# Narrow attentions: exponents from scores with keys on partitions in place of transposed probabilities

## The reference, cut to what matters

```
s = q k^T * scale + mask        # 256 x keys; keys = 768 in L0 (context and x), 512 in L2 and L3
p = exp(s - rowmax(s)) / rowsum
a = p v                         # 256 x 16
x = x + (a Wo + bias)           # in L2 times tanh(gate)
```

## Time and profile before

| | us |
|---|---|
| median of 3 runs | 1140.93 |
| lowest, highest | 1139.70, 1142.56 |
| profiled execution, span | 1145.1 |
| TensorE busy | 956.2 (84%) |
| TensorE weight loads busy | 806.1 (70%) |
| VectorE busy | 823.1 (72%) |
| ScalarE busy | 606.0 (53%) |
| GpSimd busy | 331.5 (29%) |

### The profile page before, as it was taken

How to read it: one execution, slowest core, us unless ns; L and a number is a source line. 1 busy time by engine, 2 the same in 40 slices (tenths; PEclk the granted TensorE clock), 3 DMA queues, 4 the chain that set the end, 5 groups by cost and what they waited for, 6 DMA issues and landing times. The chain is left out here.

```text
span 1145.1 us, 17853 instructions
## 1 busy us (share of the span) xinstructions
PE 956.2 (84%) x6548; PEld 806.1 (70%) x6548; DVE 823.1 (72%) x1627; ACT 606.0 (53%) x1371; POOL 331.5 (29%) x324
## 2 busy tenths in 40 slices
PE   4788886569999999975999999998586798478958
PEld 3666665557888888963898899887475466465647
DVE  3377757976787887776678878777674587747865
ACT  2488873034555555642455556554424587257842
POOL 4245541441112222004102222200005355525520
PEclk8889998878999999997999999999798699789989
DMA  5985106140001110003101111000304920195120
GB/s 176 234 143 61 16 1 253 46 153 1 21 18 38 38 38 1 1 1 117 38 1 37 38 37 38 1 1 1 116 1 111 177 43 1 51 187 73 21 79 19
DMA packets 38242, 69.49 MB, mean 61 GB/s; under 512 B 7462, under 2 KB 23336, under 8 KB 35596
## 3 DMA queue, kind: packets, MB, share of 16 engines
q1 hardware_dynamic: 38156, 68.35, 24.6%
HBM read 57.31 MB, written 11.02 MB: 60 GB/s over the span
## 5 line engine op out<-in xcount | busy, mean ns | idle before, releaser
L1189 ACT CAST L1a_probsT_hi<-L1a_bank 128x512 fp32r<-128x512 f32 x128 | 68.8, 589 | 92.6 <-PE L1a_bank L1085 92.6
L1043 POOL TENSOR_SCALAR L1a_wo_hi<-L1a_stage 128x512 fp32r<-128x512 f32 x16 | 11.3, 707 | 347.8 <-PE L1a_sums L84 336.8
L1279 DVE TENSOR_REDUCE L1a_top<-L1a_scores 128x2 f32<-128x1024 f32 x64 | 78.2, 1222 | 35.2 <-PE L1a_scores L84 35.2
L1215 ACT ACTIVATE L1a_probs<-L1a_scores,L1a_neg_max 128x512 f32<-128x512 f32 x128 | 86.8, 684 | 30.3 <-DVE L1a_bias_shifted L1283 24.7
L82 PE MATMUL L1a_bank<-L1a_probsT_hi,L1a_v_hi 128*128 128x256 f32 x256 | 72.5, 283 | 11.7 <-DVE L1a_probsT_lo L1238 11.0
L1238 DVE TENSOR_TENSOR L1a_probsT_lo<-L1a_bank,L1a_probsT_hi 128x512 fp32r<-128x512 f32 x128 | 81.9, 681 | 0.1
L1191 ACT ACTIVATE L1a_attended_hi<-L1a_bank,L1a_cols 128x256 fp32r<-128x256 f32 x64 | 30.3, 474 | 91.5 <-PE L1a_bank L84 91.5
L82 PE MATMUL L1a_bank<-L1a_w_hi,ctxT_hi 128*128 128x256 f32 x256 | 75.7, 296 | 0.0
L83 PE MATMUL L1a_bank<-L1a_w_lo,ctxT_hi 128*128 128x256 f32 x256 | 73.1, 286 | 0.0
L84 PE MATMUL L1a_bank<-L1a_w_hi,ctxT_lo 128*128 128x256 f32 x256 | 73.0, 285 | 0.0
L400 POOL TENSOR_SCALAR L0a_probs<-L0a_probs,L0a_inverse 128x768 f32<-128x768 f32 x64 | 57.2, 906 | 53.2 <-DVE L0a_inverse L651 53.2
(11 more groups left out here) (407 smaller groups left out, 3157.9 us busy)
## 6 DMA issues: line engine op xcount, KB each, us to landing
L1a_stage<-in_L_w SPq DMA_DIRECT2D x14, 1024.0 KB, 4.8
L0m_fold_wq<-in_L_wq SPq DMA_DIRECT2D x2, 2048.0 KB, 20.4
L0a_k_stack<-L0a_k_dram SPq DMA_DIRECT2D x12, 192.0 KB
L0a_w_qkv<-L0a_k_dram SPq DMA_DIRECT2D x12, 192.0 KB
L0a_probs<-in_L_wo SPq DMA_DIRECT2D x1, 2048.0 KB, 10.0
L0a_probsT<-in_L_wo SPq DMA_DIRECT2D x1, 2048.0 KB, 11.2
L0m_stage<-in_L_wm SPq DMA_DIRECT2D x4, 512.0 KB, 6.0
L0m_fold_bias_k<-in_L_bias_k SPq DMA_DIRECT2D x2, 1024.0 KB, 16.0
```

Of the source, the lines that this page charges most:

```text
L1189: nc.scalar.copy(out, source).then_inc(ring.hi_done, 1)
L1215: nc.scalar.activation(probs[:, g % 2, qt, :], scores[:, qt, :], ACT.Exp, bias=neg_max[:, g % 2, qt:qt + 1], accum_out=row_sum[:, g % 2, q ...
L1279: link(nc.vector.tensor_reduce(top[:, :], scores[:, :, :], AX.X, ALU.max))
```

## The change

The 32 heads are handled as 16 *pairs* (`NP`), two of them a unit. For each pair TensorE makes the scores twice. *Row scores* (`row_scores`) have queries on partitions as before, but contract 64 rows for each head of the pair, into two banks of a pair; VectorE takes the maxima of both heads in one instruction and nothing else uses them. *Exponents* (`exponents`) have keys on partitions: k_stack is the stationary operand, q_stack (256 queries) the moving one. The two rows 64a+33 and 64a+34 of q_stack hold the negated maxima's high and low part, against ones in k_stack, so the maximum is subtracted within the matmul, and the mask row comes the same way. ScalarE takes the exponential of 1024 elements at once, straight into `probsT`, as `product_v` reads it. The unused columns of `v` hold ones, so the product has the row sums in its row 16; after it come a copy (`take_sums`), a shuffle and a reciprocal (`invert_sums`), a product on GpSimd, and the high and low parts.

The maxima of a unit are split in high and low part, transposed (`turn_maxima`), copied, and brought into q_stack by four DMAs of two partitions. Row scores run four pairs ahead (`LEAD`). All four octets have k and q stacks of their own, and GpSimd clears each half separately; in L0a the fourth k stack still lies over w_qkv. `probsT` for two of four pairs lies over kT. PSUM: two banks for v jobs, maxima, V products and outputs (`late`), and three pairs of banks shared in turn by row scores and exponents. Two of the v jobs stay ahead, the others go between the first row scores; output blocks 0 and 1 go into the loop (`OUT_STEP`). The wide weights for the bias values are loaded in three pieces instead of two.

```diff
-        score_slots, probs_slots, small_slots = (4, 8, 8) if nk == S else (2, 6, 8)
-        probs = ph.sb("probs", [P, probs_slots, nk])
+        kept = 3 if cfg["bias_values"] else 4
+        stacks = [place(f"k_stack{o}", [P, 4, nk], F32R) for o in range(kept)]
+        if kept < OCTETS:
+            stacks.append(place("k_stack3", [P, 4, nk], F32R, at=at_w))
+        q_stack, _ = place("q_stack", [P, OCTETS, 4, Q], F32R)
+        banks = ph.psum(2)
+        pairs_banks = [ph.ctx.enter_context(nc.psum_tensor(f"{name}_pair{i}", [P, 2, 512], F32)) for i in range(3)]
+        ring = ph.ring([*banks, pairs_banks[2][:, 0, :], pairs_banks[2][:, 1, :]])
+        late = Ring(banks, ph.sem, "late")
...
+        STEPS = range(-LEAD, NP + 1)
+        def rows_of(s):
+            return [(s + LEAD, qt, c) for qt in range(2) for c in range(MC)] if s + LEAD < NP else []
+        def exps_of(s):
+            return [(s, h) for h in range(HALVES)] if 0 <= s < NP else []
+        def turned(s):
+            m = s + LEAD
+            return m // 2 - 1 if m % 2 == 0 and 2 <= m <= NP else None
+        def summed_up(s):
+            return s // 2 - 1 if s % 2 == 0 and s >= 2 else None
...
             for o in range(OCTETS):
...
                 sp.wait_ge(written[o], 64 if o else 80)
-                sp.wait_ge(cleared[r], 3)
-                if o >= 2:
-                    sp.wait_ge(scores_full, 16 * (o - 1))
+                sp.wait_ge(cleared[o], 6)
...
+            for u in range(UNITS):
+                late.wait_evacuated(sp, late_job["N", u])
+                for i in range(4):
+                    tt, a = divmod(i, 2)
+                    o, t = divmod(2 * u + tt, 4)
+                    row = 64 * a + 33
+                    sp.dma_start(raw(q_stack[row:row + 2, o, t, :]), maximaT[2 * i:2 * i + 2, u % 2, :]).then_inc(maxima_loaded[u % 2], 16)
...
+            def clear(o):
+                if o == 3 and kept < OCTETS:
+                    pool.wait_ge(late.full, late_job[v_jobs[-1]] + 1)
                 for a in range(2):
+                    half = np.s_[64 * a + 32:64 * a + 64]
+                    settled(nc.gpsimd.memset(raw(q_stack[half, o, :, :]), 0.0), cleared[o], 3 * a + 1)
+                    settled(nc.gpsimd.memset(raw(k_stack[o][half, :, :]), 1.0), cleared[o], 3 * a + 2)
+                    settled(nc.gpsimd.memset(raw(q_stack[64 * a + 32:64 * a + 33, o, :, :]), 1.0), cleared[o], 3 * a + 3)
+            clear(0)
+            settled(nc.gpsimd.memset(v[:, :, :], 1.0), values_set, 1)
+            settled(nc.gpsimd.memset(maxima[:, :, :, :], 0.0), maxima_clear, 1)
+            if cfg["bias_values"]:
+                pool.wait_ge(late.full, late_job["bias_values"] + 1)
+            for o in range(1, OCTETS):
+                clear(o)
+            for u in range(UNITS):
+                pool.wait_ge(inverted, 2 * u + 2)
...
+                nc.gpsimd.tensor_tensor(scaled[:, u % 2, :], summed[:, u % 2, :], inverse[:, u % 2, :],
+                                        ALU.mult).then_inc(scaled_ready, 1)
...
+            def row_scores(item):
...
+                wait_pair_free(pe, item)
+                for a in range(2):
+                    last = nc.tensor.matmul(pair_bank(item)[:, a, 0:CW], q_stack[64 * a:64 * a + 64, o, t, qt * P:(qt + 1) * P],
+                                            k_stack[o][64 * a:64 * a + 64, t, c * CW:(c + 1) * CW], start=True, stop=True)
+                last.then_inc(rows_full, 1)
+            def exponents(item):
...
+                if h == 0 and p % 2 == 0:
+                    pe.wait_ge(maxima_loaded[u % 2], 64 * (u // 2 + 1))
+                wait_pair_free(pe, item)
+                for kk in range(2):
+                    at = (2 * h + kk) * P
+                    for a in range(2):
+                        last = nc.tensor.matmul(pair_bank(item)[:, a, kk * Q:(kk + 1) * Q], k_stack[o][64 * a:64 * a + 64, t, at:at + P],
+                                                q_stack[64 * a:64 * a + 64, o, t, :], start=True, stop=True)
+                last.then_inc(exps_full, 1)
...
+            for s in STEPS:
+                for k in range(max(len(rows_of(s)), len(exps_of(s)), 1)):
+                    for item in rows_of(s)[k:k + 1]:
+                        row_scores(item)
+                    for item in exps_of(s)[k:k + 1]:
+                        exponents(item)
+                    if k == 0:
+                        for item in values_of(s):
+                            values(item)
+                        if turned(s) is not None:
+                            turn_maxima(turned(s))
+                        if summed_up(s) is not None:
+                            product_v(summed_up(s))
+                if s in (OUT_STEP, OUT_STEP + 1):
+                    output(s - OUT_STEP)
...
+                        nc.scalar.activation(probsT[p % 4][:, :, h * 512:(h + 1) * 512], pair_bank((p, h))[:, :, :],
+                                             ACT.Exp).then_inc(pair_freed((p, h)), 1)
...
+                nc.vector.tensor_reduce(parted[:, u % 2, qt, 2 * tt:2 * tt + 2, c], pair_bank(item)[:, :, 0:CW], AX.X, ALU.max,
+                                        negate=True).then_inc(pair_freed(item), 1)
...
+            def invert_sums(u):
+                late.wait_evacuated(dve, late_job["V", u])
...
+                nc.vector.stream_shuffle(spread_sums[:, :], summed[:, u % 2, :], [16] * 32).then_inc(inverted, 1)
+                dve.wait_ge(inverted, 2 * u + 1)
+                nc.vector.reciprocal(inverse[:, u % 2, :], spread_sums[:, :]).then_inc(inverted, 1)
...
+            for s in STEPS:
+                for item in rows_of(s):
+                    maximum(item)
+                if (s + LEAD) % 2 == 1 and s + LEAD < NP:
+                    split_maxima((s + LEAD) // 2)
...
+                if summed_up(s) is not None:
+                    invert_sums(summed_up(s))
+                if summed_up(s - 1) is not None:
+                    low(summed_up(s - 1))
```

More of the change, by code:

```diff
@@ L222, in narrow_attention @@
     quads = H // 4
[L223 removed]
+    UNITS = B * quads
     OCTETS = B * KT
[L225 to L264 removed]
@@ L300, in key_source @@
             return src[part][:, kt, at:at + n]
[L303 to L318, removed]
@@ L397, in _, with settled @@
-            for m in range(2 * HEADS):
-                slot, small = m % probs_slots, m % small_slots
-                pool.wait_ge(inverse_done, m // 2 + 1)
-                nc.gpsimd.tensor_scalar(probs[:, slot, :], probs[:, slot, :], inverse[:, small:small + 1], 1.0,
-                                        ALU.mult, ALU.mult).then_inc(normed, 1)
+            def settled(instruction, done, value):
+                instruction.then_inc(done, 1)
+                pool.wait_ge(done, value)
+            settled(nc.gpsimd.memset(raw(mask_row[:, :, :]), 0.0), padding_set, 1)
@@ L424, in _, with wait_late, values @@
                 last.then_inc(ring.full, 1)
-            for i, (b, t0) in enumerate(v_jobs):
-                job = v0 + i
+            def wait_late(job):
+                if job < 2:
+                    ring.wait_evacuated(pe, max(j for j in range(len(front)) if j % 4 == job))
+                late.wait_bank(pe, job)
+            def values(item):
+                b, t0 = item
+                job = late_job[item]
                 pe.wait_ge(w_lo, 3)
-                ring.wait_bank(pe, job)
+                wait_late(job)
@@ new lines, in row_scores @@
+            def row_scores(item):
+                p, qt, c = item
+                o, t = divmod(p, 4)
+                if t == 0 and qt == 0 and c == 0:
+                    pe.wait_ge(stack_loaded[o], 16 * stack_dmas)
+                if pair_job[item] == 2:
+                    for back in range(4):
+                        ring.wait_evacuated(pe, len(front) - 1 - back)
+                wait_pair_free(pe, item)
[3 more added lines that the diff above has]
+                last.then_inc(rows_full, 1)
@@ new lines, in output @@
+            def output(t):
+                job = late_job["O", t]
+                pe.wait_ge(w_lo, 5)
+                pe.wait_ge(low_done, quads * (t // 2 + 1))
+                wait_late(job)
+                for quad in range(quads):
+                    last = product3(nc, late.bank(job)[:, 0:D], [x[:, quad, t * P:(t + 1) * P] for x in attended],
+                                    [x[:, quad, :] for x in wo], quad == 0, quad == quads - 1)
+                last.then_inc(late.full, 1)
+            for item in v_jobs[:EARLY]:
+                values(item)
@@ L507, in projected @@
+            for t in (2, 3):
+                output(t)
         def projected(item):
@@ L543, in _, with high @@
+            def high(u):
+                if u == 0:
+                    act.wait_ge(written[0], 80)
+                b, quad = divmod(u, quads)
+                act.wait_ge(scaled_ready, u + 1)
```

(14 more changed lines are left out.)

444 lines of the change are left out of this document (251 added, 193 removed).

## The result

The changed kernel takes **1279.22 us** (median of 4 runs, 1276.88 to 1282.9) against 1141.47 for the kernel before (4 runs, 1139.70 to 1142.56): ratio 1.1206, interval 1.1174 to 1.1237, 138 us slower. The direction is as forecast and the time lies in the range, but 59 us above the forecast. The profiled execution spans 1281.0 us at a mean granted clock of 0.832.

A forecast was written before the change was run, and what follows sets the result against it. The prediction took the stack loads ahead of the maxima as deciding, then instruction order within units. L2a +26, L3a +27 and L0a +25 made +78: 1141+78=1219, rounded to 1220 us, range 1170 to 1285.

The forecast's parts named there:

- The term that decides: Stack loads: SyncE issues all four octets before the maxima, so L2a's maxima land at 928.5, L3a's exponents start at 1055.
- octet 1 lands as before, at 73: L0a's loads: octet 1 at 73, the next two at 86.4 and 99.8, first exponents at 100.3.
- the small transfers pass the stacks: Rival on SyncE's loads: maxima land 2.3 us after issue, 37 us back, 1183; chance 0.12.
- taken as 0.35: VectorE's reciprocal of 256 elements in each unit: 0.35 us, as other such operations; 1.8 us a unit kept for the range.
- slow reciprocal: Rival on VectorE's reciprocal: 1.8 us more in each of 24 units, 43 us, 1263; chance 0.08.
- stays, 1.93: TensorE's V product in each unit: unchanged at 1.93 us in L2a and 2.80 in L0a.
- clock: Rival on TensorE's clock: at 0.50 through the loops V and fills double, 66 us in all, 1286; chance 0.12.
- the forecast's 9.4: VectorE's round for one unit of L2a: 8.9 to 10.0 us, taken as 9.4; before, 10 to 11 a unit.
- the order decides, not the sums: Unit loop: alternating banks, with V between an even step's first and second, set VectorE's round: 9.4 us L2a, 12.6 L0a.
- row groups side by side: TensorE's score matmuls on 64 rows: two row groups run together, a fill takes 0.25 us, against 0.47 one by one.
- one by one: Rival on TensorE's row groups: no overlap, all units at their slow end, +9 us, 1229; inside the forecast's own 0.58.
- Faster: Rival: maxima pass the stacks, banks never couple, a unit costs VectorE's own 6.3 us (9.1 in L0a); 1121, chance 0.06.

The follow-up runs named there:

- Run 1: Changed kernel with SyncE issuing the first units' maxima ahead of octets 2 and 3, the rest interleaved; 1210.46 us.
- run 2: Changed kernel with VectorE's 128x256 reciprocal replaced by a copy, leaving out the division by the row sums; 1247.84 us.
- Run 3: Changed kernel with 12 unread filler matmuls of 256 columns on TensorE in odd steps, where it waits for VectorE; 1267.04 us.
- run 8: Run 7 without the filler: changed kernel with SyncE's new order, V last and the later reciprocal; 1202.55 us.
- run 7: Changed kernel with the edits of run 1 and run 6 plus filler matmuls (in L0a at two fills, ten each); 1194.23 us.
- run 9: Run 1 with V cut into key tiles, one behind each fill; sums, reciprocal and parts later, ScalarE's high part ahead of its sums wait; 1174.09 us.
- run 10: Run 9 with the filler matmuls in the odd steps; 1161.85 us.
- run 5: Changed kernel with the edits of run 1, run 2 and Run 3 together, division left out; 1165.57 us.
- run 4: Changed kernel with TensorE doing a unit's V product behind the second fill of its step, not between the two; 1277.61 us.
- run 6: Changed kernel with V behind the second fill and shuffle, reciprocal, high and low parts one step later; 1270.89 us.
- run 12: Run 10 with, in each tail, 28 filler matmuls before output 2 and the last unit's reciprocal ahead of the previous low part; 1148.10 us.
- run 11: Run 10 with a copy in place of the reciprocal, division left out; 1145.61 us.

## Why the prediction was right, and where it was short

**Right: the loads.** "The term that decides" was read off as 36.9 us from first score to first exponents in L2a and measured as 37.7; in L3a 36.1 and 38.9. Run 1 shows that it is the order of the queue: 69 of the 138 us come back when the maxima are issued ahead of octets 2 and 3. L0a began its exponents at 106.4, not 100.3. The step missed there is "octet 1 lands as before, at 73": the first score that needs it came at 77.9, and the first exponents 28.4 us behind that, where the forecast had 27.3. The later clearing of octet 3 (GpSimd ends it at 79.2, SyncE issues the octet from 79.3 on) cost nothing, since the DMA engines were full all the time, at 115 GB/s:

```profile
77.91 0.69 PE L536 MATMUL L0a_pair<-L0a_k_stack,L0a_q_stack 64*128 64x384 f32 x2 [7.26 <-DMA L0a_k_stack<-L0a_mask_dram]
```

```profile
62.00:98.00 36.00, 8.06 (x50) 5.21 (x50) 13.74 (x23) 2.30 (x7) 9.08 (x6) 0.66 1.08 115
```

The rival in which the small transfers pass the stacks is refuted.

**Short: the unit.** From the first exponents to the last V the forecast had 69.65 us in L2a and L3a and 94.25 in L0a (its sums plus the last exponential, 1.05, which it counts in the tail). It was 78.7, 77.8 and 110.6. That is 34 of the 57 us by which the three stages together ran past the forecast. The tails from that V on give 14 (12.7, 14.1 and 14.4 us in place of 8.85, 8.85 and 9.55) and the starts 9. Two steps failed:

- *The reciprocal "taken as 0.35".* It takes 1.75 us. The step that misled is the inference from the 128x2 reciprocal (154 ns in the narrow attentions, 166 in the wide one), which costs as much as any operation of that size: at two elements the cost of each element doesn't show. From 2 to 256 elements it is (1753-166)/254, 6.2 ns for each further element; for the copy of run 2, beside a plain operation of 128x2 (163 ns), it is (294-163)/254, 0.5. The "slow reciprocal" rival, given 0.08, was true; it priced 43 us, and 31 were measured on the path. The Trainium skill (VectorE: DVE Perf Modes, Walkthrough: the 8-slice pipeline in each mode) says that the reciprocal runs as an iterated divide with a repeat count of 8. The trace agrees in kind, with 6.2 ns against 0.5 for each element, and the page speaks for the upper end of the forecast's two values.
- *V "stays, 1.93".* Its instructions stayed; the clock under them didn't. In L2a's loop the granted clock was 0.70 on average, a mixture of the levels 0.50 (1.2 GHz) and 1.00 (2.4 GHz), and seven of L2a's eight V products took 2.9 to 3.6 us. The "clock" rival, given 0.12, was true in kind and too dear: it put 66 us on it, since it took every unit at 0.50. The reason given against it, 2 to 3 us of dense work in every unit, did not hold. Run 3 got back 12 us; the filler was worth 8 between runs 8 and 7 and 12 between runs 9 and 10.

*Luck.* Run 3 has units of 9.3 to 9.6 in L2a, which looks like the forecast's 9.4, but with 1.4 us more for the reciprocal in them than the forecast had. So the rest of its round was some 1.4 us too dear (an estimate from these two numbers), and the two errors cancel there. Nor do its terms give what it says: as written they add to 8.45 to 9.85 in L2a (not 8.9 to 10.0) and to 12.5 to 13.3 in L0a (not 12.0 to 13.3). The time is inside the range, but the range was drawn for one rival at a time. The slow reciprocal and the clock, each at its stated price, would have given 1220+43+66=1329, outside it.

So two rivals held at once with the forecast. What the runs took back singly is 69 for the order of the loads, 31 for the reciprocal and 12 for the clock, and run 5 took back 114 with all three. The remaining 24 were not separated. Part of them is in the tails, where the windows of the last two outputs have granted clocks of 0.56 to 0.63.

**Right: "the order decides, not the sums".** V as a block does close the banks for VectorE. But the order had to change at three places at once. Runs 4 and 6 took one or two of them and gave nothing clear of noise and 8 us; run 9 also split V and freed ScalarE's high part, and gave 36. Which of the two does it was not tried singly.

**Right: row groups side by side.** In run 3 the four exponent matmuls at 1010.56 are followed by the next fill at 1010.80, 0.24 us for the fill forecast at 0.25. The "one by one" rival is refuted. **"Faster"** would have needed a unit of about 7.5 us in L2a. Run 10 reaches 7.66 in one unit and 8.3 as the mean of three, and run 12, with all the repairs, is 0.4% slower than the kernel before, not faster.

## What to carry to other kernels

Before moving loads into one long run of a queue, ask which small transfer stands behind them and who waits for it: that was half of this loss, and one list in another order undid it. Price an operation at the size at which it will be used; a tiny instance shows only its fixed cost. That an engine shows no wait in one round doesn't make it the one that sets the pace: shorten its work and see whether the loop shrinks (runs 10 and 11). Taking work off TensorE can cost its clock, and then the work that stays gets slower, too; a wait that VectorE or ScalarE has in its instruction order only changes its name when one instruction is moved.

## What the runs showed of the hardware

- On VectorE a reciprocal of 128x256 takes 1753 ns, a copy of that shape 294.
- Twelve matmuls per unit that nobody reads made the kernel 12 us faster, with V at 1.93 us in place of 3.64 and a granted clock of 0.94 in place of 0.70 in L2a's loop.
- While the stacks are loaded, in pieces of 16 partitions, all DMA engines are full and move 115 GB/s in L0a and 116 in L2a in the changed kernel, and 119 to 134 in L2a before. Nothing is lost by them when they run beside the loop (run 1: 75.9 us against 75.6).
- With the reciprocal replaced by a copy, VectorE's work in L2a's loop fell from 46 to 38 us and the loop stayed at 59.4 and 59.7 us (runs 10 and 11).
